# The last eight steps of an AdaLN block on one core: a new order of the queues, and the last attention product in two column halves

## What is computed

```python
mod = (silu(c) @ wmod).reshape(4, 6, 1, 512)      # sa, ca, ga, sb, cb, gb
ga, gb = bounded away from 0 by 0.25              # gates
h = layernorm(x) * (1 + ca) + sa                  # x: 4 batches x 1024 tokens x 512, f32
q, k = h @ Wq.T, h @ Wk.T                         # 64 columns each
attn = softmax(q @ k.T)                           # the same scores for all 16 heads
x = x + ga * ((attn @ (h @ Wv.T)) @ Wo.T)
h = layernorm(x) * (1 + cb) + sb
x = x + gb * ((h @ sum_r factors[r]) / sqrt(8) + bias)
```

## Time and profile before

| | |
|---|---|
| median of three runs | 472.34 us (471.0 to 473.41) |
| profiled execution, its time | 470.67 us |
| its span, first to last instruction | 468.9 us |
| TensorE busy | 452.3 us (96%) |
| VectorE busy | 363.8 us (78%) |
| ScalarE busy | 331.7 us (71%) |
| GpSimd busy | 236.5 us (50%) |
| granted TensorE clock | 1.000 |

### The profile page before, as it was taken

One profiled execution on the slowest core, in us unless ns is written; L12 is line 12 of the kernel. 1 busy time (PEld: TensorE's weight loads), 2 busy tenths in 40 slices (PEclk: granted clock), 3 DMA queues, 4 the chain that ended last, 5 costly groups with the idle time before them and its releaser, 6 DMA issues. The chain is left out here.

```text
span 468.9 us, 7428 instructions
## 1 busy us (share of the span) xinstructions
PE 452.3 (96%) x2114; PEld 363.9 (78%) x2114; DVE 363.8 (78%) x637; ACT 331.7 (71%) x662; POOL 236.5 (50%) x307
## 2 busy tenths in 40 slices
PE   8999889999999999999999999999999989999896
PEld 3776668878887888888888888887888867777674
DVE  2887886769868778888887977887887578786665
ACT  2896755687867788787888777877787476567551
POOL 0226643561444655555555645454554576566662
PEclk9999999999999999999999999999999999999999
DMA  8968999914468457677768375868774237575612
GB/s 304 388 228 221 185 181 182 196 48 114 137 182 272 136 176 208 210 221 216 227 193 250 91 220 170 257 180 241 222 232 118 91 113 226 158 219 181 167 61 92
DMA packets 78201, 88.07 MB, mean 188 GB/s; under 512 B 4937, under 2 KB 55881, under 8 KB 78161
## 3 DMA queue, kind: packets, MB, share of 16 engines
q1 hardware_dynamic: 74208, 80.00, 56.1%
q0 software_dynamic: 3808, 7.34, 9.4%
q10 hardware_dynamic: 144, 0.26, 0.2%
HBM read 53.49 MB, written 34.10 MB: 187 GB/s over the span
## 5 line engine op out<-in xcount | busy, mean ns | idle before, releaser
L1338 POOL TENSOR_SCALAR ve<-mv 128x1 f32<-128x1 f32 x64 | 22.0, 343 | 171.4 <-DVE mv L1078 117.5
L449 PE MATMUL ps_o<-v_lo,pt_hi 128*128 128x512 f32 x256 | 100.1, 391 | 1.1 <-DVE pt_lo L967 1.1
L451 PE MATMUL ps_o<-v_hi,pt_hi 128*128 128x512 f32 x256 | 99.7, 389 | 0.0
L450 PE MATMUL ps_o<-v_hi,pt_lo 128*128 128x512 f32 x256 | 99.6, 389 | 0.0
L967 DVE TENSOR_TENSOR h_lo<-h_f,h_hi 128x512 fp32r<-128x512 f32 (+1 forms) x67 | 48.0, 716 | 13.4 <-ACT h_hi L685 12.9
L449 PEld LDWEIGHTS ps_o<-v_lo,pt_hi 128*128 128x128 f32 x256 | 48.1, 188 | 12.7 <-issue 2.5
L451 PEld LDWEIGHTS ps_o<-v_hi,pt_hi 128*128 128x128 f32 x256 | 48.0, 188 | 10.1
L450 PEld LDWEIGHTS ps_o<-v_hi,pt_lo 128*128 128x128 f32 x256 | 48.1, 188 | 9.7
L714 ACT ACTIVATE h_f<-x1b,mod_t 128x128 f32<-128x128 f32 x120 | 53.0, 595 | 3.1 <-DVE x1b L1096 3.0
L449 PE MATMUL ps_y<-f_lo,h_hi 128*128 128x512 f32 (+1 forms) x124 | 48.7, 392 | 2.9 <-ACT ffn L824 1.6
L451 PE MATMUL ps_y<-f_hi,h_hi 128*128 128x512 f32 (+1 forms) x124 | 47.9, 386 | 0.0
(11 more groups left out here) (180 smaller groups left out, 1025.5 us busy)
## 6 DMA issues: line engine op xcount, KB each, us to landing
x_blocks<-xn SPq DMA_DIRECT2D x50, 256.0 KB, 2.6
p_blocks<-probs SPq DMA_DIRECT2D x24, 512.0 KB, 3.4
pb<-p_blocks SPq DMA_DIRECT2D x96, 128.0 KB, 3.2
x_ring<-in_x SPq DMA_DIRECT2D x16, 512.0 KB, 3.9
x1b<-x_blocks SPq DMA_DIRECT2D x30, 256.0 KB, 2.8
result<-x_ring SPq DMA_DIRECT2D x15, 512.0 KB, 3.0
f_sum<-in_factors POOLq DMA_DIRECT2D x14, 512.0 KB, 6.0
wmod<-in_wmod SPq DMA_DIRECT2D x12, 512.0 KB, 6.8
```

What stands on the lines that cost most here:

```text
L449: nc.tensor.matmul(acc, a_hi, b_lo, start=first, stop=False)
L450: nc.tensor.matmul(acc, a_lo, b_hi, start=False, stop=False)
L451: return nc.tensor.matmul(acc, a_hi, b_hi, start=False, stop=last)
L1338: nc.gpsimd.tensor_scalar(ve[:, one], mv[:, u, 1:2], EPS, None, ALU.add).then_inc(ve_done, 1)
```

## The change

It has six parts. (1) ScalarE's `ffn_out(20)` in step 23 stands ahead of the pair of queries, which waits for scores. (2) In closing steps ScalarE normalizes tile t-1 behind `modulate_x1(t-2)` and `h2_upper(t-2)`; in step 24 the exponentials stand ahead of `h2_upper`. (3) VectorE makes the first half of `probs_rest(t)` ahead of `add_x(t-1)` and the second half ahead of `x1_stats(t-1)`; in step 30 `h2_rest` goes ahead of `turn_p`. (4) SyncE issues `fetch_x1(t-1)` behind `send_p(t+2)`. (5) The attention product of tile 31 is made in two halves of 256 columns, into `ps_o` and `ps_s`; VectorE gates, adds and sums each half by itself, and the transposes of tile 30 follow both halves. (6) At the end VectorE adds EPS and makes the normalized tile 31 itself, GpSimd makes only the power, and GpSimd's last two additions are in other places: that of tile 28 behind the gated bias of tile 30, that of tile 29 behind the low parts of `h2` of tile 31.

```diff
@@ SyncE, step
-                if 1 <= t < T - 1:
+                if 1 <= t < T - TB:
                     fetch_x1(t - 1, 1 - u)
                 if scored_in(t) is not None and not turned_by_pe(scored_in(t)):
                     send_p(scored_in(t))
+                if T - TB <= t < T - 1:
+                    fetch_x1(t - 1, 1 - u)
@@ TensorE
+            def last_attention(g):
+                wait(pe, attn_done, T - 1)
+                pe.wait_ge(exp_done, T)
+                first = ((g >> 2) & 1) * TB
+                for half, columns_ in enumerate(column_halves):
+                    for j in range(TB):
+                        if half == 0 and j % HALF == 0:
+                            pe.wait_ge(pt_lo_done, 2 * (T - 1) + 1 + j // HALF)
+                        v = [part[:, first + j, columns_] for part in (v_hi, v_lo)]
+                        last = three(last_attn[half][:, 0:D // 2], (pt_hi[:, j, :], pt_lo[:, j, :]), v,
+                                     j == 0, j == TB - 1)
+                    last.then_inc(o_acc, 1)
...
-                attend(t, g, transpose_last_but_one if t == T - 1 else None)
+                if t < T - 1:
+                    attend(t, g)
+                else:
+                    last_attention(g)
+                    transpose_last_but_one()
@@ ScalarE, step
+                if t == T - TB - 1:
+                    ffn_out(t - 3)
                 if queries_in(t) is not None:
                     pair_q(queries_in(t))
-                if t >= 3:
+                if 3 <= t < T - TB - 1:
                     ffn_out(t - 3)
@@ ScalarE, closing_step
                 ffn_out(t - 3)
+                modulate_x1(t - 2, batch_of((t - 2) // 2))
+                opens = t == T - TB
+                if opens:
+                    exponentials(scored_in(t))
+                h2_upper(t - 2)
                 if t == T - 1:
-                    normalize_last_x1(t - 1, 1 - u)
+                    normalize_last_but_one(t - 1, 1 - u)
                 else:
                     normalize_x1(t - 1, 1 - u, False)
-                modulate_x1(t - 2, batch_of((t - 2) // 2))
-                h2_upper(t - 2)
-                if scored_in(t) is not None:
+                if scored_in(t) is not None and not opens:
                     exponentials(scored_in(t))
...
-            normalize_last_x1(T - 1, 1)
@@ VectorE
+            def last_half_of_x1(half):
+                columns_ = column_halves[half]
+                tile = x_ring[:, 2 * TB - 1, columns_]
...
+                dve.wait_ge(o_acc, T + half)
+                nc.vector.scalar_tensor_tensor(out=attn[:, columns_], in0=last_attn[half][:, 0:D // 2],
...
+                nc.vector.tensor_tensor(tile, attn[:, columns_], tile, ALU.add).then_inc(x1_done, 1)
...
+                nc.vector.bn_stats(stats2[:, half, :], tile).then_inc(stats2_done, 1)
+
+            def last_moments():
+                dve.wait_ge(stats2_done, T + 1)
+                nc.vector.bn_aggr(mv2[:, 1, :], stats2[:].rearrange("p h s -> p (h s)")).then_inc(mv2_done, 1)
...
+                nc.vector.tensor_scalar(ve2[:, 1:2], mv2[:, 1, 1:2], EPS, None, ALU.add).then_inc(ve2_done, 1)
+
+            def normalize_last_x1():
+                dve.wait_ge(rstd2_done, T)
+                dve.wait_ge(h2_ps, 1)
+                nc.vector.tensor_scalar(xn[:], x_ring[:, 2 * TB - 1, :], mv2[:, 1, 0:1], rstd2[:, 1:2],
+                                        ALU.subtract, ALU.mult).then_inc(x2n_done, 1)
@@ VectorE, closing_step
+                probs_rest(t, 0)
                 add_x(t - 1)
+                probs_rest(t, 1)
                 x1_stats(t - 1, 1 - u)
-                probs_rest(t, 0)
-                probs_rest(t, 1)
                 turn_x1(t - 2)
...
                 if scored_in(t) is not None:
                     row_max(scored_in(t))
-                if t + 1 < T:
                     turn_p(t + 1)
-                h2_rest(t - 2)
-                gate_attention(t, u, B - 1)
+                    h2_rest(t - 2)
+                elif t + 1 < T:
+                    h2_rest(t - 2)
+                    turn_p(t + 1)
+                if t < T - 1:
+                    gate_attention(t, u, B - 1)
+                else:
+                    last_half_of_x1(0)
+                    h2_rest(t - 2)
+                    last_half_of_x1(1)
+                    last_moments()
@@ VectorE, end
-            add_x(T - 1)
-            x1_stats(T - 1, 1)
             h2_rest(T - 2, to=h2_parts_of[1], whole=h_f)
+            normalize_last_x1()
@@ GpSimd, end
-            result(T - 4)
+            add_bias(T - 4)
+            gate_result(T - 4, B - 1)
             add_gated_bias(T - 2)
-            of_x1(T - 1, 1)
+            wait_alone(pool, pool_passed, gated_done, T - 3)
+            add_result(T - 4)
+            pool.wait_ge(ve2_done, T)
+            nc.gpsimd.tensor_tensor(rstd2[:, 1:2], ve2[:, 1:2], minus_half[:], ALU.pow).then_inc(rstd2_done, 1)
             pool.wait_ge(ffn_done, T - 2)
+            pool.wait_ge(h2_lo_done, T + C - 1)
             wait_alone(pool, pool_passed, bias_added, 2)
             add_result(T - 3)
```

More of the change, by code:

```diff
@@ L204, in adaln_block @@
         last_banks = [ps_y, ps_o]
+        last_attn = [ps_o, ps_s]
         wvo_banks = [ps_v, ps_o, ps_y, ps_qk]
@@ L532, in transpose_probs, with attend @@
                 transposes(ps_t[1], probs, HALF, HALF).then_inc(pt_ps, 1)
-            def attend(t, g, aside=None):
+            def attend(t, g):
                 pe.wait_ge(v_lo_done, (g >> 2) * TB + TB)
@@ L539, in attend @@
                 for j in range(TB):
-                    if j == 3 * TB // 4 and aside is not None:
-                        aside()
                     if j % HALF == 0:
@@ L789, in normalize_x1, with normalize_last_but_one @@
                                      scale=rstd2[:, u:u + 1], bias=nmr2[:, u:u + 1]).then_inc(x2n_done, 1)
-            def normalize_last_x1(t, u):
+            def normalize_last_but_one(t, u):
                 act.wait_ge(nmr2_done, t + 1)
[L793 to L796, removed]
+                act.wait_ge(x2n_out, 16 * t)
                 nc.scalar.activation(xn[:], x_ring[:, t & (2 * TB - 1), :], ACT.Identity,
@@ L1063, in gate_attention @@
                                                op1=ALU.mult).then_inc(attn_done, 1)
+            def last_half_of_x1(half):
+                columns_ = column_halves[half]
+                tile = x_ring[:, 2 * TB - 1, columns_]
+                dve.wait_ge(gate_loaded[0], 16 * B)
+                dve.wait_ge(rden_done, T)
+                dve.wait_ge(o_acc, T + half)
+                nc.vector.scalar_tensor_tensor(out=attn[:, columns_], in0=last_attn[half][:, 0:D // 2],
+                                               scalar=rden[:, 1:2], in1=gates[:, 0, (B - 1) & 1, columns_],
+                                               op0=ALU.mult, op1=ALU.mult).then_inc(attn_done, 1)
+                dve.wait_ge(attn_done, T + half)
+                nc.vector.tensor_tensor(tile, attn[:, columns_], tile, ALU.add).then_inc(x1_done, 1)
+                if half == 0:
+                    dve.wait_ge(mv2_done, T - 1)
+                dve.wait_ge(x1_done, T + half)
+                nc.vector.bn_stats(stats2[:, half, :], tile).then_inc(stats2_done, 1)
+            def last_moments():
+                dve.wait_ge(stats2_done, T + 1)
+                nc.vector.bn_aggr(mv2[:, 1, :], stats2[:].rearrange("p h s -> p (h s)")).then_inc(mv2_done, 1)
+                dve.wait_ge(mv2_done, T)
+                dve.wait_ge(rstd2_done, T - 1)
+                nc.vector.tensor_scalar(ve2[:, 1:2], mv2[:, 1, 1:2], EPS, None, ALU.add).then_inc(ve2_done, 1)
[4 more added lines that the diff above has]
+                                        ALU.subtract, ALU.mult).then_inc(x2n_done, 1)
             def add_x(t):
```

## The result

The changed kernel takes 478.52 us (median of 6 runs, 476.21 to 480.97) against 472.65 us (median of 6): a ratio of 1.0133, with a 95% interval of 1.0106 to 1.0161. It is 1.3% slower, where I had forecast 471.4 and given "slower by over 0.5%" a chance of 0.06.

What follows compares the result with a forecast made beforehand. Three loops, each about as long as TensorE's own work, bound it (probabilities: 9.52 us a step). Steps to 29 0.0 to -0.3, in all -1.0 at the last transposes, +0.1 at the end: -0.9, 472.34 to 471.4 us; range 469.2 to 473.6.

Steps and rivals of the forecast that it cites:

- landing 2.8: Last batch: x1's fetch lands 2.8 us after issue; extremes of 2.6 and 3.1 move four rounds by -0.8 and +1.2.
- x1's trip: Closing steps: x1's send, fetch, transpose and modulation; had slack before, and its later start pays for the new order.
- round of 9.33 us: Steps 25 to 29: modulation, normalization, send, fetch, landing and transpose take 9.33 us a step; 0.3 us gain left by step 29.
- Rival C: Closing steps: x1's send, fetch and landing become the bound, a round is 9.97 us, total 474.3 us; chance 0.13.
- The hole of 0.84: Step 24: TensorE's 0.84 us wait for ffn_out goes, putting TensorE 0.8 us ahead at the step's start.
- The lock at h2_rest: Closing steps: GpSimd's pass blocks VectorE's h2_rest, making hit gates 0.6 to 1.0 us late; two hits in five steps.
- Rival D: Closing steps: GpSimd's pass hits every step, gates 10.1 us apart instead of 9.6, total 473.9 us; chance 0.05.
- The gate-to-exponentials leg: Closing steps: gate to end of exponentials takes 8.77 us against 8.99, gaining 0.22 per two steps, without waiting for nmr.
- -1.0 at the last transposes: End: TensorE's last transposes come at 459.2 against 460.19, 1.0 us earlier.
- The last attention product 1.0 earlier: Step 31: last attention product at 447.4 instead of 448.43, its 0.51 us hole gone; range 446.5 to 448.5.
- Part 6: End: holding back add_result(29) delays the 512 KB store of pair 14; charged 0.1 us, bound 1.0.
- rival E: End: no change, the gain eaten by the late store or add_result(28), total 472.3 us; chance 0.10.

Runs made afterwards that it cites:

- the end alone: Kernel before plus halved last attention product, VectorE's normalization and GpSimd's moved passes with the late addition; steps 24 to 30 as before: 472.42 us, ratio 1.0008.
- the new orders in the last two steps: Kernel before with the end's edits and add_result(29) not held back, plus VectorE's and ScalarE's new orders in steps 30 and 31 only: ratio 0.9974.
- The queue alone: Kernel before with only SyncE's new order, fetch_x1 behind send_p in the last batch: 473.00 us, ratio 1.0002.
- part 1 alone: Kernel before with only ffn_out(20) moved ahead of the queries: 473.71 us, ratio 1.0031.
- normalization-first kernel: Changed kernel with ScalarE's closing order undone, normalization again ahead of modulation: 477.88 us, ratio 1.0107.
- the store behind the fetch: Changed kernel with the 512 KB store of a finished pair issued behind fetch_x1 in steps 24 to 31: 474.28 us, ratio 1.0034.
- the fetch ahead of `send_p`: Changed kernel with SyncE's order undone, fetch_x1 again ahead of send_p: 477.65 us, ratio 1.0095.

## Why the prediction was wrong

**The step that failed** is the term "landing 2.8" in x1's trip, and with it the round of 9.33 us and its bounds of 2.6 and 3.1. Those numbers were measured where at most the store stood ahead of the fetch, 2.0 to 2.6 us earlier, and the probabilities behind it. The edit that I was pricing puts the probabilities ahead of it too, so that in odd steps 1 MB is issued in the 2.2 us before it. I wrote down both moves of the queue, and charged SyncE's order for what it did to `send_p` alone. The measured landing was 3.7 in the median and 5.7 at most; the rounds from modulation to modulation, from step 25 on, were 12.6, 10.4, 10.4, 11.2 and 10.3 us instead of 9.33. The four rounds that I counted took 44.6 instead of 37.3: 5.6 of these 7.3 us are landings beyond 2.8 (5.7, 2.7, 3.7, 4.7), and 1.2 is the modulation of step 27 behind `ffn_out`. The trip also started 0.8 later than I had it (`x1b` turned at 383.0 on the clock of before, against 382.2), which goes with part 1's slow cast. Moving the store, which my text names only at the end of the kernel, brings back 6.7 of the 8.3 us that A to C grew by.

**Rival C** was the right mechanism ("x1's trip becomes the bound"), with a chance of 0.13 and a price of 474.3. It was too small for the same reason, and because a second effect stood behind it: TensorE's waits of 3.2 and 2.3 us were followed by spells at the lower clock, about 3.0 us in the profiled execution. No rival had a clock term, although C itself made TensorE wait.

**Part 1.** The hole of 0.84 went, as said: the feed-forward product of step 24 starts 0.79 behind A instead of 1.87. It was not only handed back through `x1b`; alone it cost 0.8 from A to B (ratio 1.0031), through GpSimd's pass beside a cast. I had looked for the lock at `h2_rest` only.

**The lock at h2_rest** was a worry in the wrong place. Of eight `h2_rest` in the closing steps after, four took 1.08 to 1.25 us and none 1.5; above the 0.69 of a free one they cost 2.1 us together, against 9.9 us of waits for `x1b`. In the kernel before, the same count over its free 0.65 gives 3.3, so the lock cost less than before. I had two hits in steps 25 to 29; there was one over 1.0 us (1.14). Rival D did not occur.

**The gate-to-exponentials leg** went as predicted in its parts (no wait for `nmr`, the same passes ahead of `turn_x1`, what is late next is `x1b`), and the gain was never seen because `x1b` was later than any of it.

**Step 30 and 31, part 5.** -1.0 at the last transposes, by themselves, was right: A to B is 1.2 shorter with the end alone. The last attention product 1.0 earlier came true only with the new orders in the last two steps (0.9), and then bought nothing that the runs show.

**Part 6.** Charged 0.1 with a bound of 1.0; measured 1.2. This was rival E's mechanism, a mis-sized term: the late addition cancels the end's gain. I had looked only at the store that it moves, not at VectorE's addition, which it holds for 0.6.

**What stays open.** The landing of 5.7 us in step 25 and of 4.7 in step 28 is longer than the bytes ahead explain. In the transfer rates from 398 to 408 us (40 slices of 0.25 us) the transfers run at 200 to 434 GB/s from 398.5 to 403.25, and then the queue crawls at 8 to 16 GB/s for a microsecond:

```profile
GB/s 0 10 266 272 307 355 395 377 311 360 393 324 348 352 336 319 242 201 266 340 434 82 16 16 8 8 61 250 258 225 295 291 213 123 295 103 12 20 0 0
```

Step 27 has the same order of issues and a landing of 3.7, and steps 24 and 26 that of step 28 and landings of 2.7. What holds the last packets was not found. Part 3, VectorE's new order, was never run by itself. The queue alone (1.0002), part 1 alone (1.0031) and the end alone (1.0008) come to 1.0041, and the normalization-first kernel, which adds only VectorE's order, to 1.0107; how the rest splits between the later `nmr`, the landing of `x1b` and the clock was not tried apart. The late normalization was not run by itself either. The 3.0 us of the clock come from the count of slow matmuls in one execution, not from a run of its own.

## What to carry to other kernels

Price a moved DMA at its new place in the queue: list the bytes issued between the transfer that it depends on and itself, stores included, and give its landing a bound from a place with as much ahead of it, not from its old one. A move that costs nothing by itself (the queue's order, 1.0002) can use the slack that another move counts on (the late normalization; together with the rest 1.0133), so sum what all moves take from a slack before calling any free. Unurgent stores go last in a queue, but not so late that they meet the final ones.

## What was not expected of the hardware

A cast of 64x256 elements from SBUF to SBUF, one input, took 1.28 us instead of 0.29 when it began inside a GpSimd pass. The lock at `h2_rest` is one of two inputs, and I had taken one-input instructions to be free of it. By the Trainium skill, SBUF — State Buffer, section "SBUF: two separate sides", a VectorE instruction in a 2-port mode is subject to the same exclusion. The rows of part 1 alone fit that (the cast ended 0.15 after the pass); that the cast runs in such a mode, no run here shows.

Waits of TensorE of 3.24 and 2.26 us in the changed kernel, and of 2.25 with normalization first, were each followed by about 3 us at half the clock, with matmuls 0.43 apart instead of 0.23. Waits of up to 1.6 us with the store behind the fetch, and of up to 1.85 with the fetch ahead of `send_p`, were followed by none.
